# Loads at the ends of two attention layers go to ScalarE's queue; squares, and one more row tile, move in the projection

## What is computed

```python
def _gat_layer(x, W, adj):
    Wh, Ws = jnp.split(x @ W, 2, axis=-1)
    a = jax.nn.softmax(Wh @ Ws.T, axis=-1) * adj
    return jax.nn.leaky_relu(a @ Wh + x, 0.01)

y = x
for l in range(2):
    y = _gat_layer(y, W_stack[l], adj)
x = _layernorm(x + y)
ba = jnp.maximum(jnp.sign(x), 0.0)
x = _layernorm(x + jax.nn.relu(adj @ (ba @ jnp.sign(weight).T)))
```

## Time and profile before

| | us |
|---|---|
| median of 3 runs | 2148.17 (2147.42 to 2153.5) |
| the profiled execution | 2151.31 |
| its span | 2149.4 |
| PE busy in it | 2110.1 |

### The profile page before, as it was taken

The page is one execution under the profiler, slowest core; times in us unless marked ns, Lnnn a source line. Parts: engine busy times, 40 slices in busy tenths (PEclk is TensorE's granted clock), DMA queues, the critical chain, the costliest instruction groups (busy, mean ns, idle before and its releaser), DMA issues.

```text
span 2149.4 us, 38691 instructions
## 1 busy us (share of the span) xinstructions
PE 2110.1 (98%) x13260; PEld 1295.3 (60%) x13260; DVE 1592.3 (74%) x4057; ACT 908.2 (42%) x2047; POOL 689.5 (32%) x623
## 2 busy tenths in 40 slices
PE   6999999999999999999999999999999999999998
PEld 2456666666666666664446666666666666665444
DVE  7987877788877778876986776776677776767465
ACT  5764344444444444443765344344434443443000
POOL 2853223232223233222863232333323332322000
PEclk9999999999999999999999999999999999999999
DMA  7998878788878687769998987888878978779794
GB/s 216 213 222 155 175 154 164 157 155 161 169 151 166 154 165 159 161 138 236 204 211 183 184 162 165 162 167 172 168 155 171 169 161 181 158 157 220 218 304 133
DMA packets 779526, 380.18 MB, mean 177 GB/s; under 512 B 642880, under 2 KB 701376, under 8 KB 777664
## 3 DMA queue, kind: packets, MB, share of 16 engines
q1 hardware_dynamic: 768512, 341.89, 73.8%
q0 software_dynamic: 3328, 22.16, 7.0%
q10 hardware_dynamic: 7488, 13.63, 1.8%
HBM read 206.24 MB, written 59.11 MB: 123 GB/s over the span
## 4 chain that ended last, share of the span: by engine, by line
PE 91%; DVE 3%; DMA 2%; issue 1%; ACT 1%; SPq 1%; POOL 0%; DVEq 0%; ACTq 0%; POOLq 0%
PE banks L1157 38%; PE banks L1126 31%; PE banks L783 10%; PE banks L1661 7%; PE banks L1135 3%; DMA adj_rows_a<-adj_rows 1%; PE banks L1115 1%; PE banks L605 1%; DVE halves_a L1385 1%; DMA values<-x_rows 0%; DMA probs_t_a<-halves_a 0%; DVE row_a L1340 0%; SPq L1002 0%; DVE adj_low L1453 0%; DVE w_p L725 0%
## 5 line engine op out<-in xcount | busy, mean ns | idle before, releaser
L1157 PE MATMUL banks<-values,probs_t_a 128*128 128x512 f16 x4056 | 961.2, 380 | 7.3 <-DMA probs_t_a<-halves_a 4.2
L1323 POOL TENSOR_TENSOR row_a<-row_a,adj_rows_a 128x512 f32<-128x512 f32 (+1 forms) x364 | 456.7, 1269 | 1163.7 <-ACT row_a L1245 1133.6
L1157 PEld LDWEIGHTS banks<-values,probs_t_a 128*128 128x128 f16 x4056 | 397.3, 98 | 382.2 <-issue 9.6
L1237 ACT ACTIVATE row_a<-banks 128x256 f32<-128x256 f32 x468 | 177.3, 379 | 628.6 <-PE banks L1126 609.1
L1126 PE MATMUL banks<-keys_t,q_even_a 128*128 128x256 f16 x3528 | 430.9, 273 | 1.8 <-DVE peaks_a L1340 1.1
L1385 DVE SCALAR_TENSOR_TENSOR halves_a<-row_a,halves_a 128x512 f16<-128x512 f32 (+1 forms) x364 | 272.5, 749 | 192.1 <-ACT halves_a L1260 189.7
L1126 PEld LDWEIGHTS banks<-keys_t,q_even_a 128*128 128x128 f16 x3528 | 343.8, 98 | 102.5 <-DVE peaks_a L1340 4.9
L1126 PE MATMUL banks<-keys_t,q_odd_a 128*128 128x256 f16 x3024 | 370.0, 273 | 4.4 <-DVE peaks_a L1340 1.8
L1245 ACT ACTIVATE row_a<-row_a,shift_a,scales 128x512 f32<-128x512 f32 (+1 forms) x364 | 281.4, 774 | 174.0 <-DVE shift_a L1375 173.9
L1126 PEld LDWEIGHTS banks<-keys_t,q_odd_a 128*128 128x128 f16 x3024 | 294.3, 98 | 92.1 <-DVE peaks_a L1340 6.0
L1407 DVE SCALAR_TENSOR_TENSOR acc_a<-acc_a,factor_a,banks 128x512 f32<-128x512 f32 x312 | 232.8, 746 | 106.1 <-PE banks L1157 99.3
(11 more groups left out here) (131 smaller groups left out, 1482.7 us busy)
## 6 DMA issues: line engine op xcount, KB each, us to landing
adj_rows_a<-adj_rows SPq DMA_DIRECT2D x312, 256.0 KB, 3.2
adj_t<-adj_blocks POOLq DMA_DIRECT2D x104, 208.0 KB, 3.9
keys_t<-adj_t SPq DMA_DIRECT2D x26, 832.0 KB, 7.9
x_rows_a<-x_rows SPq DMA_DIRECT2D x52, 256.0 KB, 3.6
s_rows<-sum_rows_p SPq DMA_DIRECT2D x24, 512.0 KB, 3.1
values<-x_rows SPq DMA_DIRECT2D x13, 512.0 KB, 5.4
adj_rows_a<-adj_rows SPq DMA_DIRECT2D x52, 128.0 KB, 2.7
x_mid<-x_rows_a SPq DMA_DIRECT2D x26, 256.0 KB, 3.4
```

Of the source, the lines that this page charges most:

```text
L1157: last = pe.matmul(out_bank(u), probs_t[:, turned_slot(w), u, ph * tiles + j, :], values[:, 4 * step_of(w) + j, vh, :], start=(j == 0 and ...
L1237: act.activation(quarter(w, u, odd), as_quarter(bank(w, SET_A)), ACT.Copy).then_inc(scores_copied, 1)
L1323: pool.tensor_tensor(piece, piece, adj_rows[:, n % ADJ_RING, 0:width(w)], ALU.mult).then_inc(masked, 1)
```

## The change

- `FILL = 5` row tiles instead of four are halved ahead of the projection's loop, in both layers; in the loop ACT and DVE work on row tile 2i+5 and 2i+6 instead of 2i+4 and 2i+5. In layer 0 DVE's low half of tile 4 stands inside `scale_layer`. In layer 1 the high halves stand in windows 91 to 95, one in each, instead of four in window 91.
- In layer 0's start ACT squares rows 2 and 3, before it waits for the scale of W; DVE scales them ahead of the rests of W, and ACT's high half of tile 2 stands between the two sides of W.
- `load_x` of windows 88 to 93, `send_w_peak`, `fetch_w_peaks`, `gather_low_bits`, `load_products` and `load_adj16` of the windows are issued by ACT, at the end of its own pass through the same windows, instead of by SP.

```diff
-RING, X_RING = 4, 3
+RING, X_RING, FILL = 4, 3, 5
@@ scale_layer
         dve.reduce_max(facts[:, 5:6], norms2[:], AX_X).then_inc(norm_peak, 1)
+        if layer == 0:
+            x_lo_half(dve, 4)
         dve.wait_ge(norm_all, layer + 1)
@@ project, act_program
-            n = t if t < 2 else 2 + (t - FIRST) // 2
+            n = t if t < FIRST else FIRST + (t - FIRST) // 2
...
             x_hi_half(act, 1)
+            square_rows(2)
+            square_rows(3)
             act.wait_ge(w_scale_ready, layer + 1)
             for side in (0, 1):
                 for c in range(DC):
                     halve_w(c, cols_of(side))
-            x_hi_half(act, 2)
+                if side == 0:
+                    x_hi_half(act, 2)
             square_rows(FIRST)
             x_hi_half(act, 3)
             for t in range(FIRST + 2, T, 2):
                 square_rows(t)
+            x_hi_half(act, 4)
...
-                if 2 * i + RING + two < T:
-                    x_hi_half(act, 2 * i + RING + two)
+                if 2 * i + FILL + two < T:
+                    x_hi_half(act, 2 * i + FILL + two)
@@ project, dve_program
             scale_w(dve)
+            dve.wait_ge(squared, FIRST)
+            scale_rows(dve, slice(2, FIRST))
             for side in (0, 1):
                 for c in range(DC):
                     lo_w(c, side)
-            square_rows(2)
-            square_rows(3)
-            scale_rows(dve, slice(2, FIRST))
             x_lo_half(dve, 2)
...
-                if 2 * i + RING + two < T:
-                    x_lo_half(dve, 2 * i + RING + two)
+                if 2 * i + FILL + two < T:
+                    x_lo_half(dve, 2 * i + FILL + two)
@@ attend, sp_program
-            if ahead and piece_windows.get(w - 3, -1) == pieces - 1:
-                ahead["send_w_peak"](sp)
-            if ahead and piece_windows.get(w - 5, -1) == pieces - 1:
-                ahead["fetch_w_peaks"](sp)
-            if last_layer and w == 5:
-                binary["gather_low_bits"](sp)
...
-                ending = w - (windows - STEPS)
-                if 2 <= ending < 5:
-                    binary["load_products"](sp, ending - 2)
-                elif ending in (5, 6, 12, 13):
-                    n = (5, 6, 12, 13).index(ending)
-                    binary["load_adj16"](sp, 2 * n)
-                    binary["load_adj16"](sp, 2 * n + 1)
...
-                behind = w - (windows - STEPS) - LAG - 1
-                if 0 <= behind < WIDE:
-                    ahead["load_x"](sp, 2 * behind)
-                    ahead["load_x"](sp, 2 * behind + 1)
@@ attend, act_program, at the end of window w
-            if ahead and w == windows:
-                for t in range(RING):
-                    ahead["x_hi_half"](act, t)
+            if ahead and 0 <= w - windows < FILL:
+                ahead["x_hi_half"](act, w - windows)
+            behind = w - (windows - STEPS) - LAG - 1
+            if ahead and 0 <= behind < WIDE:
+                ahead["load_x"](act, 2 * behind)
+                ahead["load_x"](act, 2 * behind + 1)
+            if ahead and piece_windows.get(w - 3, -1) == pieces - 1:
+                ahead["send_w_peak"](act)
+            if ahead and piece_windows.get(w - 5, -1) == pieces - 1:
+                ahead["fetch_w_peaks"](act)
+            if last_layer and w == 5:
+                binary["gather_low_bits"](act)
+            ending = w - (windows - STEPS)
+            if last_layer and 2 <= ending < 5:
+                binary["load_products"](act, ending - 2)
+            elif last_layer and ending in (5, 6, 12, 13):
+                n = (5, 6, 12, 13).index(ending)
+                binary["load_adj16"](act, 2 * n)
+                binary["load_adj16"](act, 2 * n + 1)
```

More of the change, by code:

```diff
@@ L755, in dve_program @@
                 square_rows(t)
-            dve.wait_ge(squared, 2 + (T - FIRST) // 2)
+            dve.wait_ge(squared, FIRST + (T - FIRST) // 2)
         scale_rows(dve, slice(early, T))
@@ L1094, in sp_program @@
                     store(t)
-                behind = w - (windows - STEPS) - LAG - 1
-                if w >= windows and w - windows < RING:
+                if 0 <= w - windows < RING:
                     ahead["turn_x"](sp, w - windows)
-                if 0 <= behind < WIDE:
-                    ahead["load_x"](sp, 2 * behind)
-                    ahead["load_x"](sp, 2 * behind + 1)
     def sign_bank(t):
@@ L1517, in dve_program @@
                     ahead["scale_early_rows"](dve)
-                if 0 <= w - windows < RING:
+                if 0 <= w - windows < FILL:
                     ahead["x_lo_half"](dve, w - windows)
```

## The result

The changed kernel takes 2172.75 us (median of 5 runs, 2168.98 to 2175.12), the kernel before 2149.87 beside it (5 runs, 2147.42 to 2153.5): a ratio of 1.0102, 95% interval 1.0086 to 1.0117. The forecast was 2141.0, with 2149.5 as the upper end. The sign was wrong, and the time lies 23 us outside the range.

The account below looks back on a forecast made before the run. PE was taken as the bound, busy 2110 of 2149 us, so only its idle times and clock count; 2.4 - 3.4 - 4.9 - 0.7 - 0.6 = -7.2 us gave 2141.0 us against the median of 2148.17, range 2135.5 to 2149.5.

Parts of the forecast that it names:

- the five places named: Layer 0's start, the projection's loop, both layers' window ends and small transfers; elsewhere PE was said to have no idle time.
- Term 1, the start: Layer 0's start: tile 4 begins earlier, tile 6 later with a clock drop; +2.4 us, bounds -0.7 and +3.5.
- the fixed one: At layer 0's start, POOL's wait is a code load, so its sums keep their time; following the copies would add 0.9 us.
- Term 2, the ring: Projection loop, both layers: from one `keys_hi_half` to the next 9.8 us, under PE's 10.4 per pair, so cost 0.
- The rival of a ring that outruns PE: Projection loop: the ring exceeds PE's 10.4 us, some 9 pairs in each layer wait 0.9 us; 2157 us, chance 0.12.
- Term 3, the layer-0 end: End of layer 0's windows: x loads issued earlier from ACT shorten PE's 3.04 us wait; -3.4 us, bounds 0 and -4.7.
- Term 4, the layer-1 end: End of layer 1's windows: ACT's earlier product and `adj` loads free the last transposes; -4.9 us, bounds -1 and -5.9.
- Term 5, small transfers: Moved to ACT: `send_w_peak` -0.7 us (0 to -1.6), `gather_low_bits` -0.6 us (0 to -0.85).
- The queues do not matter: A transfer costs the same from either queue, so waits at both window ends shrink only by earlier issue; 2146.6 us, chance 0.23.
- The two faster rivals: Queues not mattering (2146.6 us, chance 0.23), and layer 0's start costing nothing, tile 6 keeping its time (2138.6 us, chance 0.13).
- the two slower ones: The projection's ring outruns PE (2157 us, chance 0.12); ACT's loads hold up exponentials in nine windows (2150 us, chance 0.04).

Follow-up runs that it names:

- start_alone: The kernel before with only the squares and FILL = 5 as changed, all DMAs on SP: 2154.76 us, ratio 1.0016.
- tile_four: `loads_later` with only row tile 4 of layer 0 halved ahead of the loop and tile 6's transpose ahead of `turn_keys(0)`: 2146.59 us, ratio 0.9975 to the kernel before.
- act_from_91: The changed kernel with the x loads of windows 88 to 90 back on SP, those of 91 to 93 on ACT: 2166.54 us, ratio 1.0074 to before.
- loads_later: The kernel before, only SP's order changed: window 89 loads no x, layer 1's second two `adj` tiles stand behind the last transposes: 2145.72 us, ratio 0.9977.
- small_on_act: `loads_later` with `send_w_peak`, `fetch_w_peaks` and `gather_low_bits` on ACT: 2145.19 us, ratio 0.9976 to the kernel before.
- small_packets: The changed kernel with each pair of layer 1's x loaded in two column halves, packets of 1 KB instead of 2 KB: 2170.83 us, ratio 1.0098 to before.
- hold_loads: The changed kernel with ACT's x loads of windows 91 to 93 waiting for their window's turned row tile: 2175.57 us, ratio 1.0120 to the kernel before.
- act_to_90: The changed kernel with the x loads of windows 91 to 93 back on SP, those of 88 to 90 on ACT: 2160.76 us, ratio 1.0043 to before.

## Why the prediction was wrong

**What bounds the kernel**: right that an edit counts only where it moves PE's idle times and its clock. But the five places named don't hold all: 1.7 us stand at the attention's start, and 0.9 drifted in before 494 us.

**Term 1, the start** (+2.4; found +1.6 at row tile 6 and +1.7 at the attention's start, 3.3 in all): right in most of its steps, and ended too early. Evictions began at 37.52 (forecast 37.65), PE began tile 4 at 41.31 (41.35) after 1.50 us and with no drop of the clock, and POOL's sums began at 41.22 (41.20). POOL stood 7.08 us between its all-reduce and its first sum (6.83 in the earlier trace rows), and the sums didn't move with the copies, which came 0.8 us later. The Trainium skill (GPSIMD Engine Reference, Instruction dispatch) has the first call of a freshly loaded function pay about 6 us for loading its code. The trace agrees: of the two cases that the forecast set apart, the fixed one came. Tile 6 started at 54.73 (55.5) after 2.90 us (3.7); the 0.7 us for DVE's value halves weren't there; the clock's 1.7 were in this execution, while that of `start_alone` had 2.91 us idle and a clock of 1.00 behind it. What the term left out is the attention's start, where SP issued `turn_keys` at 148.40 instead of 144.32, and PE's wait for DVE's peaks rose from 0.55 to 2.28 us.

**Term 2, the ring** (9.8 us, cost 0): right in the ring's length, wrong that it costs nothing. From one `keys_hi_half` to the next it took 9.8, 9.8, 10.0 and 10.1 us between 75 and 115 us, and PE had no idle time until the windows. But a ring only 0.3 to 0.6 us shorter than PE's 10.4 can't catch up as before's did (9.3), and leaves a lag at its end. `tile_four`, which keeps before's order behind tile 4, waits 0.55 us at the attention's start; `start_alone`, which changes it, waits 2.54. That is where these 1.7 us come from, and the two runs show the order to be the cause, though not each link of it. The rival of a ring that outruns PE didn't occur.

**Term 3, the layer-0 end** (-3.4, found +17.4): this step failed. Its premise was "5 to 7 us earlier, and no longer ahead in the same queue". The first half holds (985.37, where before has 987.56 and the changed kernel is 4.3 us late by then: 6.5 us earlier). But 6.5 us earlier is 0.4 us ahead of the transposes of the window, which SP's loads had stood behind: the busiest stretch, not "a quieter stretch". And the step took a transfer's slowness beside another queue from the earlier trace rows, 7.0 us against 2.0, for a transfer of its own kind. For SP's transposes, which move 256 bytes when ACT moves 2 KB, it was 10.5 and 16.9 us, where the same two took 8.1 and 4.1 before. The second mistake is one of order: "its chain hangs on the same DVE sum and moves with it" was said of x's tile 0 of layer 1. In SP's program `turn_x` stood among the loads, at most two of them ahead of the next transpose; on ACT six loads had no such neighbour, and about two thirds of the loss are theirs (`act_from_91`). The forecast counted the waits that the moved instruction brings, and not the order that it takes away.

**Term 4, the layer-1 end** (-4.9, found +3.0): failed in the same way. The wait at the last window went as forecast, and was replaced one window earlier by 4.24 us and a longer stretch of the lower clock, because the loads now stood ahead of those transposes. "What is late next" was sought on ACT (0.5) and at the sign products (0.5), not in the transposes of the window before.

**Term 5, small transfers** (-0.7 and -0.6): `gather_low_bits` brought the 0.4 us of its wait (0.85 to 0.45), `send_w_peak` nothing (1.57 against 1.40). The first was right within 0.2, the second came out at its upper bound, 0. The 0.9 us that the table adds in that stage are about what equal code drifts by: `loads_later`, unchanged up to there, moves by 1.0 us against before between row tile 6 and 494 us. So neither 0.4 nor 0.9 us can be told from drift in one trace, and `small_on_act` has no difference that can be told. No cause was looked for.

**The rivals.** "The queues do not matter" came nearest in sense, though its 2146.6 is 26 us short: moving bulk to another queue brings no bandwidth. The Trainium skill (DMA: Bandwidth & Descriptors, Issuing engines are not separate DMA queues) says that only the issue time is saved. The traces agree so far, and go further: over 11 to 12 us beside the transposes the changed kernel moved 166 GB/s at a DMA share near 1, the kernel before 226, with the same mix (2192 of 2885 packets under 512 bytes, and 2888 of 3800), so here bandwidth was lost. The Trainium skill (DMA: Bandwidth & Descriptors, Queues, rings and completion order) says that each engine takes packets from the queues in turn. The one-for-one counts of `small_packets` agree with it where both queues are full. The forecast had not drawn the consequence: taken in turn, the queue with the small packets gets few bytes, 0.13 MB of 1.14 in those 3 us. The stretches are these, of the changed kernel and of the kernel before (length, busy us, clock, DMA share, GB/s):

```profile
985.00:997.00 12.00, 6.88 (x32) 2.76 (x29) 5.11 (x17) 2.41 (x7) 1.91 (x4) 1.00 0.97 166
...
978.00:989.00 11.00, 9.91 (x52) 4.90 (x50) 5.97 (x17) 3.04 (x8) 2.92 (x5) 1.00 1.08 226
```

Why the total falls, and not only SP's share of it, no run here tells apart.

**The range and the chances.** The two faster rivals were bounded by waits that the trace of before shows, and the two slower ones were sought in the projection and in ACT's own stream (2150, one sentence, chance 0.04). No case let a moved load make another transfer later than it was, though the earlier trace rows had shown a factor of 3.5 for such a pair.

## What to carry to other kernels

A DMA that is moved to another queue loses its place in an order. Before such a move, list what stood behind it and ahead of it in the old queue, and ask what now keeps it from running beside, or ahead of, those. In this kernel, loads of MB and the transposes that PE waits for belong in one queue, with the loads placed behind the transposes that are needed next: that order alone brought 0.23%, and the second queue for the loads of x cost 0.6 to 0.9%. A pipeline that just keeps up was not free either: it handed its lag on to the next stage (2.28 us of idle time where 0.55 had been). And a stage's gain or loss in one trace is sure to two or three microseconds at best, as equal code drifted by that much between two traces.

## What the runs showed of the hardware that was not expected

- Where two queues of plain and transposing DMAs were both busy, they passed packets one for one: 525 of 2 KB beside 524 of 256 bytes, and 1139 of 1 KB beside 1144. Other stretches aren't so: 399 of 2 KB beside 582 in 3 us of the changed kernel, and 3347 of 512 bytes beside 1572 in the 9.5 us from 1988.5 on. The first transpose of x of layer 1 took 16.9, 12.2 and 11.3 us beside 3 MB in 2 KB packets, 9.7 beside the same in 1 KB packets, and 3.8 with none beside it.
- SP's issues themselves slowed down: the first three transposes of x took SP 4.37, 4.26 and 6.65 us to issue beside ACT's loads and the fourth, behind them, 1.23; the same four in the kernel before took 1.2 to 2.9 us.
- How long TensorE's clock stays low isn't told by the idle time. Around idle times of 2.90, 4.24, 6.40 and 9.52 us it was 0.50 for 3.4, 6.8, 6.8 and 10.2 us in the changed kernel; but around 2.93 us for 6.8 (`act_from_91`), around 3.76 for 6.8 (`hold_loads`), and around 4.64 (`act_to_90`) and 4.89 (`start_alone`) for 3.4. After 1.50 us it stayed at 1.00. Between 2 and 3 us the idle time alone doesn't settle whether it falls at all: behind 2.03 us it fell; behind 2.13 us at the same tile in `loads_later` it didn't, as these two lines of PE's timeline and of its stretches show, nor behind 2.28 us in the changed kernel and 2.91 in `start_alone`. So the 1.7 us that the forecast put on each idle time over 2 us are a chance in this range, not a price.

```profile
41.28 10.53 PE L783 MATMUL banks<-w_p,x_t_p 128*128 128x512 f16 x48 [2.13 <-DMA x_t_p<-x_p]
...
41.29:44.70 3.41, 3.41 (x16) 1.57 (x17) 2.12 (x2) 0.66 (x2) 3.33 (x3) 1.00 0.37 68
```
